# Attention with a routed mixture of experts: routing weights carried with the rows and applied to each expert tile's output

## The chip, the cores and the metric

The program runs on one core of one Trainium2 chip. The core has five engines that run side by side and meet only at semaphores: TensorE (PE, with its weight loads as PEld), VectorE (DVE), ScalarE (ACT), GpSimd (POOL) and SyncE (SP, which issues most transfers). The metric is the time in microseconds of one execution on the device; lower is better.

## The reference, cut to what matters

The input is 4 batches of 1,024 tokens with 256 values each. A layer norm gives `xn`. One branch is causal attention with 16 heads and a linear decay. The other is a mixture of 8 experts, of which each token takes two. The output is `x + s * silu(experts)`.

```python
probs = softmax(x @ gate_w)
gate_score, gate_idx = top_k(probs, 2)
gate_score = gate_score / sum(gate_score)
combine = einsum('tk,tke->te', gate_score, onehot) * alpha
h = gelu(einsum('th,ehi->eti', x, fc1_w) + fc1_b)
y = einsum('eti,eih->eth', h, fc2_w) + fc2_b
out = einsum('eth,te->th', y, combine)
...
x = x + s * silu(out)
```

So the sum over experts has two terms for each token, each the output of one chosen expert times one weight (`gate_score` times that expert's `alpha`).

## The kernel before, in words

**Three stages.** From the start to about 522 us the kernel does the layer norm, the projections and the attention, in 16 windows of four heads; beside the first windows it chooses the experts. From about 522 to 667 us it runs the experts. Until 710 us it adds up: the last projection of the attention, the two weighted expert rows of each token, silu, product, input.

**Routing and scatter (attention stage).** The 4,096 tokens are 32 tiles of 128. `weight[:, t, k]` holds the weight of the token's k-th expert, `slot[:, t, k]` the row of a sorted list in DRAM, `xs_dram`, in which the rows of one expert stand together and each expert begins at a multiple of 128 rows. GpSimd loads two or three token tiles into `x_move` (L897), writes the number of each row's place in `y_dram` into column 0 (L880), and sends one indirect DMA for each tile and k (L885): each row goes to its slot. A row of `xs_dram` is W = 257 words wide: the number, then the 256 values. `scatter(q, k)` paces these DMAs by the exponentials of the window q. The places between the experts' rows are cleared with a row `blank` whose number points to spare rows (`clear_pads`, L859).

**Experts.** There are SLOTS = 71 tiles of the sorted list. The order on each engine is written out by `skewed`: for each n it calls the named functions for tile n plus an offset.
- SP: `load_tile(n)` (L662 to L666) loads a tile into one of four buffers, when TensorE has transposed tile n - 4 and VectorE has taken its row numbers. SP's other loads and stores of this stage stand between these (L683 to L704).
- TensorE: `x_transpose(n + 3)` (L1677), `hidden(n + 2)` (L1694), `expert_out(n)` (L1716). `hidden` waits for the copied weights of the tile's expert (`w1_ready`), `expert_out` for gelu and for the output evacuation two tiles earlier (`y_out`).
- VectorE: `take_row(n + 3)` copies the column of row numbers into `y_row_of` (L1368); `h_evacuate(n + 2)` reads the tile's expert number into a register and adds that expert's bias while it moves the product from PSUM (L1374); `y_evacuate(n)` reads the number again and does the same for the second product into one of 8 buffers `ysb` (L1414). From tile 15 on, nine steps that split the output bias into three bfloat16 parts stand behind it (L1381 to L1400); tile 12 has an inversion of the attention's last sums before it.
- ScalarE: `x_evacuate(n + 3)` (L1009), `gelu(n + 2)` (L1013), `take_weights(n + 4)` (L1020), which copies the next expert's first weights.
- GpSimd: for each tile one indirect DMA from `ysb` to the rows of `y_dram` (L912), when `row_taken` and `y_out` allow. Beside 24 tiles (12 to 19, 31 to 38, 50 to 57) it first does one step of the attention's normalisation (`normalise`, L868), and eight such steps ahead of tile 0.

**Final sum.** SP waits until all stores to `y_dram` have landed, and then issues eight loads of `y`, each with the two expert rows of 256 tokens (0.52 MB), and further ones as `gsum_done` counts on; each output of 0.26 MB is stored behind `fin_done` (L715 to L720). There are 16 pairs of token tiles. For pair m:
- ScalarE: `scale_first(m)` multiplies the first row by its weight, two activations of 128x256 (L1040); `silu(m)` (L1046). `in_turn` sends `scale_first` two pairs ahead.
- VectorE: `add_second(m)` multiplies the second row by its weight and adds it, two instructions of 128x256 (L1429); `product(m)` multiplies with the attention's projection in PSUM (L1439); `add_input(m)` adds x (L1444). The order is `product(m)`, `add_second(m + 2)`, `add_input(m)`.
- TensorE: a bias matmul and eight more for each pair (L1737, L1742) into one of four banks, so it may be four pairs ahead of `product`.

## Time and profile before

| | |
|---|---|
| median of 3 runs | 706.29 us (703.04 to 708.08) |
| the profiled execution's own time | 712.01 us |
| its span | 710.2 us |
| granted TensorE clock, mean | 0.986 of full speed |
| busy: PE, PEld | 681.3 us, 451.7 us |
| busy: DVE, ACT, POOL | 536.2, 484.1, 239.9 us |
| packets of DMA | 74802, 124.46 MB |

The span is the profiled time from the first to the last instruction; the execution's own time has the work around it too. A row in the order of time gives the start in us, the duration in us, the engine, the line, the operation, what it writes `<-` what it reads, and in brackets how long the engine sat idle before and what ended that idle time. In the durations of VectorE the last 0.08 us or so overlap the next instruction if that has nothing to wait for, so the distance from start to start is what one costs. A time to landing counts from a transfer's issue to its last byte.

### The profile page before, as it was taken

The page shows a single profiled execution, that of the slowest core. Times are in us where ns is not written, and L with a number is a line of the kernel's source. Part 1 is how long each engine was busy: PE and PEld are TensorE (multiplying, and loading weights), DVE is VectorE, ACT ScalarE, POOL GpSimd, SP SyncE. Part 2 cuts the span into 40 slices and gives each one's busy share as a digit, 9 for nine tenths or more (in the row PEclk, how much of TensorE's full clock was granted, in tenths as well). Part 3 has the DMA queues.
Part 4 walks back from the last instruction along what each step waited for, and adds up shares of the span by engine and source line. Part 5 has one row for each costly group of instructions (what it writes and reads, how often), then busy time and mean ns, then how long its engine had stood idle before and what let it go on. Part 6 is the DMA issues. An engine that isn't in the chain of part 4 may idle for free.

```text
span 710.2 us, 16190 instructions
## 1 busy us (share of the span) xinstructions
PE 681.3 (96%) x5367; PEld 451.7 (64%) x5370; DVE 536.2 (75%) x1146; ACT 484.1 (68%) x994; POOL 239.9 (34%) x336
## 2 busy tenths in 40 slices
PE   7998999999999999999999999999999999999985
PEld 4876666455555555555555554554469999999764
DVE  6566887999999999989999899997234554444298
ACT  3553344577787877788787777778876666666374
POOL 4261211133023433324333342310025857575300
PEclk9999899899999999999999999999999999999999
DMA  6999885243776685676568558630179686955396
GB/s 206 279 270 376 251 282 194 55 66 89 105 138 142 136 175 130 134 183 132 145 153 180 132 115 171 151 68 18 48 183 279 243 205 214 237 177 179 117 399 248
DMA packets 74802, 124.46 MB, mean 175 GB/s; under 512 B 13832, under 2 KB 44296, under 8 KB 74600
## 3 DMA queue, kind: packets, MB, share of 16 engines
q1 hardware_dynamic: 65104, 95.26, 53.2%
q0 software_dynamic: 9616, 28.17, 13.1%
q8 instruction: 44, 0.72, 0.5%
q14 instruction: 38, 0.31, 0.2%
HBM read 72.64 MB, written 49.72 MB: 172 GB/s over the span
## 4 chain that ended last, share of the span: by engine, by line
PE 79%; DVE 9%; DMA 7%; ACT 2%; issue 2%; POOL 0%; POOLq 0%; SPq 0%; DVEq 0%; ACTq 0%
PE ps L1606 19%; PE ps L1590 14%; PE ps L1537 13%; PE ps L1694 9%; PE ps L1716 9%; PE ps L1526 6%; PE ps L1489 5%; DVE mxa L1131 3%; DMA aug<-q_parts 3%; PE ps L1499 2%; DMA q_parts<-arena 2%; PE ps L1677 2%; ACT arena L992 1%; DVE arena L1439 1%; DVE x_room L1444 1%
## 5 line engine op out<-in xcount | busy, mean ns | idle before, releaser
L1131 DVE TENSOR_REDUCE mxa<-ps 128x1 f32<-128x512 f32 (+3 forms) x608 | 358.1, 654 | 36.4 <-PE ps L1526 22.2
L992 ACT ACTIVATE arena<-ps 128x512 f32<-128x512 f32 x576 | 303.0, 606 | 78.2 <-PE ps L1590 42.2
L1590 PE MATMUL ps<-aug 59*128 59x512 f32 (+3 forms) x768 | 216.6, 402 | 0.8 <-ACT arena L992 0.5
L1537 PE MATMUL ps<-aug 57*128 57x512 f32 (+3 forms) x768 | 212.1, 401 | 4.9 <-DVE mxa L1131 1.9
L1590 PEld LDWEIGHTS ps<-aug 59*128 59x128 f32 x768 | 112.4, 188 | 78.8 <-ACT arena L992 70.2
L1606 PE MATMUL ps<-arena,v_q 128*32 128x512 f32 (+3 forms) x1536 | 155.5, 500 | 1.0 <-ACT arena L992 1.0
L1537 PEld LDWEIGHTS ps<-aug 57*128 57x128 f32 x768 | 109.4, 188 | 43.4 <-DVE mxa L1131 24.8
L885 POOL DMA_INDIRECT xs_dram<-arena,slot x64 | 62.7, 980 | 75.9 <-ACT arena L992 72.6
L912 POOL DMA_INDIRECT y_dram<-arena,y_row_of x71 | 69.6, 980 | 46.8 <-DVE y_row_of L1368 38.1
L1526 PE MATMUL ps<-key_mask,key_rows 64*128 64x128 bf16 (+2 forms) x352 | 76.9, 254 | 0.0
L1694 PE MATMUL ps<-arena 128*128 128x128 f32 x568 | 75.2, 275 | 0.0
L1526 PE MATMUL ps<-query_mask,query_rows 64*128 64x256 bf16 (+1 forms) x320 | 74.8, 260 | 0.0
L1716 PE MATMUL ps<-w_sb,arena 128*128 x284 | 73.1, 380 | 0.0
L1694 PEld LDWEIGHTS ps<-arena 128*128 128x128 f32 x568 | 69.1, 192 | 0.5 <-issue 0.4
L1374 DVE TENSOR_TENSOR arena<-ps,arena 128x256 f32<-128x256 f32 x71 | 30.2, 425 | 40.4 <-PE ps L1694 40.1
L1020 ACT ACTIVATE arena<-w_sb 128x512 f32 x69 | 43.5, 630 | 21.0 <-issue 19.6
L1606 PEld LDWEIGHTS ps<-arena,v_q 128*32 128x32 f32 x1536 | 34.9, 109 | 33.0 <-issue 18.3
L1489 PE MATMUL ps<-split_room 128*128 128x512 f32 x192 | 54.2, 418 | 1.1 <-DVE split_room L1190 1.1
L1414 DVE TENSOR_TENSOR arena<-ps,arena 128x256 f32<-128x256 f32 x71 | 30.1, 424 | 33.2 <-PE ps L1716 33.1
L1716 PEld LDWEIGHTS ps<-w_sb,arena 128*128 128x128 f32 x284 | 48.7, 191 | 4.3 <-issue 0.4
L1013 ACT ACTIVATE arena<-arena 128x256 f32<-128x256 f32 x71 | 29.6, 417 | 27.4 <-DVE arena L1374 27.4
L1526 PEld LDWEIGHTS ps<-key_mask,key_rows 64*128 64x128 bf16 x352 | 30.1, 94 | 18.1 <-issue 10.5
(150 smaller groups left out, 639.3 us busy)
## 6 DMA issues: line engine op xcount, KB each, us to landing
aug<-k_parts SPq DMA_DIRECT2D x96, 128.0 KB, 4.8
aug<-q_parts SPq DMA_DIRECT2D x96, 128.0 KB, 4.5
arena<-xs_dram SPq DMA_DIRECT2D x71, 128.5 KB, 3.3
k_parts<-arena SPq DMA_DIRECT2D x16, 512.0 KB, 5.0
q_parts<-arena SPq DMA_DIRECT2D x16, 512.0 KB, 5.4
arena<-y_dram SPq DMA_DIRECT2D x16, 512.0 KB, 7.8
xn_dram<-arena SPq DMA_DIRECT2D x8, 512.0 KB, 5.3
a_dram<-arena SPq DMA_DIRECT2D x128, 32.0 KB
```

The source lines that it names most:

```text
L885: nc.gpsimd.indirect_dma_start(out=xs_dram, in_=x_move[:, s, :], in_offset=None, out_offset=bass.IndirectOffsetOnAxis(ap=slot[:, first_til ...
L912: nc.gpsimd.indirect_dma_start(out=y_dram, in_=ysb[n % STEP], in_offset=None, out_offset=bass.IndirectOffsetOnAxis(ap=y_row_of[:, n:n + 1] ...
L992: nc.scalar.activation(prob_slot(q, i), score_bank(q, i), ACT.Exp).then_inc(exp_done, 1)
L1020: nc.scalar.activation(w1_now[j % 2], w1_sb[:, bass.ds(e * KT, KT), :], ACT.Copy).then_inc(w1_ready, 1)
L1131: nc.vector.tensor_reduce(dst, src, AX.X, ALU.max).then_inc(piece_used, 1)
L1489: ins = nc.tensor.matmul(bank(4 + n % 2), w[:, k, m * P:(m + 1) * P], xT[:, k, :], start=(s == 0 and k == 0), stop=(s == 2 and k == KT - 1))
L1526: return nc.tensor.matmul(bass.AP(out_.tensor, out_.offset + first, cols), stationary[rows, :, :].rearrange("p a two -> p (a two)"), over( ...
L1537: ins = nc.tensor.matmul(banks[:, at_ * width:(at_ + 1) * width], k_aug[n][rows, hp, ib * P:(ib + 1) * P], q_aug[n][rows, hp, lo:lo + widt ...
L1590: ins = nc.tensor.matmul(out_[:, col0:col0 + hi - lo], q_aug[n][rows, h // SIDES_OF_ARRAY, jb * P:(jb + 1) * P], k_aug[n][rows, h // SIDES ...
L1606: ins = nc.tensor.matmul(bank(OUT_BANK)[2 * HD * h:2 * HD * (h + 1), lo - c * BANK:BANK], v_q[n][:, jb, h, :], prob_slot(q, i)[:, col0:col ...
L1694: ins = nc.tensor.matmul(bank(2 + j % 2)[:, m * P:(m + 1) * P], w1_now[j % 2][:, k, m * P:(m + 1) * P], xgT[j % CH][:, k * P:(k + 1) * P], ...
L1716: ins = nc.tensor.matmul(bank(6 + j % 2)[:, 0:D], hid[j % CH][:, k * P:(k + 1) * P], w2_sb[:, e * KT + k, :], start=(k == 0), stop=(k == K ...
```

## The change

1. A row of `xs_dram` is 258 words wide (`LEAD = 2`): number, weight, 256 values. `scatter` copies the weights of its tiles into column 1 with one more GpSimd copy. The two clearing patterns cover the second column.
2. `take_row` copies two words. They go to `row_and_weight`, which lies in the memory of `logits`.
3. `h_evacuate` keeps the register with the tile's expert number for `y_evacuate`, which does not read it again.
4. `y_evacuate` counts a new semaphore `y_biased` with its addition, waits for it, and multiplies the tile in place by the row's weight; `y_out` now counts the multiplication. TensorE waits for `y_biased` (it needs the PSUM bank only), GpSimd's store for `y_out`.
5. In the final sum ScalarE no longer scales; VectorE adds the two rows of a pair with one tensor_tensor of 128x512 and waits for the load of `y` itself. `in_turn` and `y_scaled` are gone.

```diff
-W = D + 1
+LEAD = 2
+W = D + LEAD
...
             def scatter(q, k):
...
+                nc.gpsimd.tensor_copy(x_move[:, 0:count, 1:2], weight[:, first_tile:first_tile + count, k:k + 1]
+                                      ).then_inc(rows_ready, 1)
+                pool.wait_ge(rows_ready, 2 * (2 * r + k) + 3)
...
-                pool.wait_ge(y_out, n + 3)
+                pool.wait_ge(y_out, n + 1)
                 nc.gpsimd.indirect_dma_start(
                     out=y_dram, in_=ysb[n % STEP], in_offset=None,
-                    out_offset=bass.IndirectOffsetOnAxis(ap=y_row_of[:, n:n + 1], axis=0)).then_inc(y_stored[n % STEP], 16)
+                    out_offset=bass.IndirectOffsetOnAxis(ap=row_and_weight[:, n, 0:1], axis=0)).then_inc(y_stored[n % STEP], 16)
...
-            def scale_first(m):
-                j = m % DEEP
-                act.wait_ge(ya_in[m % DEEP_Y], 16 * (m // DEEP_Y) + 16)
-                if m >= DEEP:
-                    act.wait_ge(sg_done, m - DEEP + 1)
-                for i in range(2):
-                    ins = nc.scalar.activation(gsum[j][:, i * D:(i + 1) * D], ya[m % DEEP_Y][:, i, 0, :], ACT.Identity,
-                                               scale=weight[:, 2 * m + i, 0:1])
-                ins.then_inc(y_scaled, 1)
...
-            in_turn(scale_first, silu)
+            for m in range(NT // 2):
+                silu(m)
...
             def take_row(n, j):
                 dve.wait_ge(xg_in[j % CH], 16 * (n // CH) + 16)
-                nc.vector.tensor_copy(y_row_of[:, bass.ds(n, 1)], x_move[:, j % CH, 0:1].bitcast(i32)).then_inc(row_taken, 1)
+                nc.vector.tensor_copy(row_and_weight[:, n, :], x_move[:, j % CH, 0:LEAD].bitcast(i32)).then_inc(row_taken, 1)
...
             def h_evacuate(n, j):
-                e = dve.value_load(tile_expert[0:1, bass.ds(n, 1)], min_val=0, max_val=E - 1)
+                e = expert_of[n] = dve.value_load(tile_expert[0:1, bass.ds(n, 1)], min_val=0, max_val=E - 1)
...
-                e = dve.value_load(tile_expert[0:1, bass.ds(n, 1)], min_val=0, max_val=E - 1)
+                e = expert_of.pop(n)
                 dve.wait_ge(l2_done, n + 1)
                 if n >= STEP:
                     dve.wait_ge(y_stored[j % STEP], 16 * (n // STEP))
-                nc.vector.tensor_tensor(ysb[j % STEP], bank(6 + j % 2)[:, 0:D], b2_sb[:, e, :], ALU.add).then_inc(y_out, 1)
+                nc.vector.tensor_tensor(ysb[j % STEP], bank(6 + j % 2)[:, 0:D], b2_sb[:, e, :], ALU.add).then_inc(y_biased, 1)
+                dve.wait_ge(y_biased, n + 3)
+                nc.vector.tensor_scalar(ysb[j % STEP], ysb[j % STEP], row_and_weight[:, n, 1:2].bitcast(fp32), None,
+                                        ALU.mult).then_inc(y_out, 1)
...
             def add_second(m):
                 j = m % DEEP
-                dve.wait_ge(y_scaled, m + 1)
-                for i in range(2):
-                    part = gsum[j][:, i * D:(i + 1) * D]
-                    ins = nc.vector.scalar_tensor_tensor(part, ya[m % DEEP_Y][:, i, 1, :], weight[:, 2 * m + i, 1:2],
-                                                         part, ALU.mult, ALU.add)
-                ins.then_inc(gsum_done, 1)
+                dve.wait_ge(ya_in[m % DEEP_Y], 16 * (m // DEEP_Y) + 16)
+                if m >= DEEP:
+                    dve.wait_ge(sg_done, m - DEEP + 1)
+                nc.vector.tensor_tensor(gsum[j].rearrange("p (t d) -> p t d", d=D), ya[m % DEEP_Y][:, :, 0, :],
+                                        ya[m % DEEP_Y][:, :, 1, :], ALU.add).then_inc(gsum_done, 1)
...
-                pe.wait_ge(y_out, n + 1)
+                pe.wait_ge(y_biased, n + 1)
```

## Rows read from the trace of the kernel before

**Rows 1.** The page's head and its busy time by engine (busy us, share, instructions).

```profile
span 710.2 us, 16190 instructions
...
PE 681.3 (96%) x5367; PEld 451.7 (64%) x5370; DVE 536.2 (75%) x1146; ACT 484.1 (68%) x994; POOL 239.9 (34%) x336
```

**Rows 2.** Busy time by stretch, expert stage: columns PE, PEld, DVE, ACT, POOL busy, PEclk, DMA share, GB/s.

```profile
560.00:600.00 40.00, 40.00 (x284) 36.93 (x283) 20.80 (x69) 26.72 (x62) 27.06 (x31) 1.00 0.72 202
```

**Rows 3.** Order of time in the expert stage: start us, us, engine, line, operation, idle before.

```profile
600.64 0.42 DVE L1414 TENSOR_TENSOR arena<-ps,arena 128x256 f32<-128x256 f32 x1 [0.44 <-PE ps L1716]
600.88 0.74 POOL L868 TENSOR_TENSOR v_all<-v_all,arena 128x256 f32<-128x256 f32 x1
...
600.98 0.14 DVE L1368 COPY y_row_of<-arena 128x1 int32<-128x1 int32 x1
...
601.75 0.42 DVE L1374 TENSOR_TENSOR arena<-ps,arena 128x256 f32<-128x256 f32 x1 [0.63 <-PE ps L1694]
601.83 1.01 POOL L912 DMA_INDIRECT y_dram<-arena,y_row_of  x1 [0.21 <-issue]
...
602.62 0.42 DVE L1414 TENSOR_TENSOR arena<-ps,arena 128x256 f32<-128x256 f32 x1 [0.44 <-PE ps L1716]
...
602.92 0.63 ACT L1020 ACTIVATE arena<-w_sb 128x512 f32 x1 [0.29 <-issue]
...
604.49 1.06 PE L1694 MATMUL ps<-arena 128*128 128x128 f32 x8
```

**Rows 4.** Busy time by stretch, final stage.

```profile
685.00:690.00 5.00, 5.00 (x24) 3.78 (x23) 5.00 (x12) 3.79 (x9) 0.00 (x0) 1.00 1.06 395
```

**Rows 5.** Order of time in the final stage, all engines.

```profile
668.36 1.89 PE L1742 MATMUL ps<-wo_sb,v_all 128*128 128x256 f32 x8
...
673.86 0.91 ACT L1040 ACTIVATE arena<-arena,weight 128x256 f32<-128x256 f32 x2 [8.64 <-DMA arena<-y_dram]
...
676.94 0.68 DVE L1439 TENSOR_TENSOR arena<-ps,arena 128x512 f32<-128x512 f32 x1
...
700.93 0.68 DVE L1439 TENSOR_TENSOR arena<-ps,arena 128x512 f32<-128x512 f32 x1
...
701.53 0.86 DVE L1429 SCALAR_TENSOR_TENSOR arena<-arena,weight 128x256 f32<-128x256 f32 x2
702.32 0.68 DVE L1444 TENSOR_TENSOR x_room<-x_room,arena 128x512 f32<-128x512 f32 x1
...
702.92 0.68 DVE L1439 TENSOR_TENSOR arena<-ps,arena 128x512 f32<-128x512 f32 x1
```

**Rows 6.** The line of GpSimd's row-number copies: duration ns min/median/max.

```profile
L880 POOL COPY arena<-y_row x22: 188/191/215, 180.9 to 456.7; 128x3 int32<-128x3 int32 x20, 128x2 int32<-128x2 int32 x2
```

**Rows 7.** Order of time of VectorE, tile that also splits the output bias.

```profile
568.14 0.42 DVE L1374 TENSOR_TENSOR arena<-ps,arena 128x256 f32<-128x256 f32 x1 [0.29 <-PE ps L1694]
```

**Rows 8.** Groups of VectorE instructions by shape: count | busy us, mean ns | idle before.

```profile
L1351 DVE COPY arena<-w_sb 128x512 f32 x2 | 0.9, 430 | 5.9 <-issue 5.9
...
L1180 DVE TENSOR_SCALAR arena<-arena,rstd,shift 128x256 f32<-128x256 f32 x2 | 0.7, 410 | 0.0
...
L1392 DVE CAST arena<-arena 128x256 bf16<-128x256 f32 x1 | 0.4, 417 | 0.0
...
L1386 DVE CAST arena<-ob_sb 128x256 bf16<-128x256 f32 x1 | 0.3, 284 | 0.0
```

**Rows 9.** The line of the tile loads (L666), of the loads issued from 579 to 582.

```profile
DMA to landing us min/median/max: 6.6/6.6/6.6
```

**Rows 10.** Order of time at the end of the expert stage.

```profile
663.70 0.42 DVE L1414 TENSOR_TENSOR arena<-ps,arena 128x256 f32<-128x256 f32 x1 [0.44 <-PE ps L1716]
...
664.88 0.96 POOL L912 DMA_INDIRECT y_dram<-arena,y_row_of  x1 [0.79 <-DVE arena L1414]
...
667.41 0.96 POOL L912 DMA_INDIRECT y_dram<-arena,y_row_of  x1 [0.30 <-issue]
```

**Rows 11.** The line of the loads of y (L706), all 16.

```profile
DMA to landing us min/median/max: 3.8/7.8/9.3
```

More of the change, by code:

```diff
@@ L227, in is_last @@
     return isinstance(q, int) and q == NQ - 1
-def in_turn(ahead, what):
-    for m in range(AHEAD_OF_PRODUCT):
-        ahead(m)
-    for m in range(NT // 2):
-        what(m)
-        if m + AHEAD_OF_PRODUCT < NT // 2:
-            ahead(m + AHEAD_OF_PRODUCT)
 def attention_moe_kernel(nc, x, wqT, wkT, wvT, woT, qb, kb, vb, ob, gate, w1, b1, w2, b2, alpha,
@@ L297, in attention_moe_kernel @@
         tile_expert = sb("tile_expert", [P, SLOTS], i32)
-        y_row_of = sb("y_row_of", [P, SLOTS], i32)
+        row_and_weight = logits[:, :, :].rearrange("p t e -> p (t e)")[:, 0:LEAD * SLOTS].bitcast(i32).rearrange("p (n r) -> p n r", r=LEAD)
         y_row = sb("y_row", [P, NT, 2], i32)
         blank = sb("blank", [P, W])
-        zeros = blank[:, 1:W]
+        zeros = blank[:, LEAD:W]
         pad_slot = sb("pad_slot", [P, E], i32)
@@ L304, in attention_moe_kernel @@
         spare = sb("spare", [P, E, 2], i32)
-        ARENA = 16 * 1024 + CH
+        ARENA = 16 * 1024 + LEAD * CH
         arena = sb("arena", [P, ARENA])
@@ L361, in attention_moe_kernel @@
         at[0] = 0
-        xg = [x_move[:, j, 1:W] for j in range(CH)]
+        xg = [x_move[:, j, LEAD:W] for j in range(CH)]
         at[0] = 0
@@ L461, in attention_moe_kernel @@
         g_done = sem("g_done"); w1_ready = sem("w1_ready"); l2_done = sem("l2_done")
-        y_out = sem("y_out"); y_stored = [sem(f"y_stored{n}") for n in range(STEP)]
+        y_biased = sem("y_biased"); y_out = sem("y_out"); y_stored = [sem(f"y_stored{n}") for n in range(STEP)]
         x_all_in = sem("x_all_in"); a_in = [sem(f"a_in{b}") for b in range(B)]
         ya_in = [sem(f"ya_in{n}") for n in range(DEEP_Y)]
-        vb_turned = sem("vb_turned"); vb_out = sem("vb_out"); vb_done = sem("vb_done"); ob_step = sem("ob_step"); ob_split = sem("ob_split"); s_proj = sem("s_proj"); y_scaled = sem("y_scaled")
+        vb_turned = sem("vb_turned"); vb_out = sem("vb_out"); vb_done = sem("vb_done"); ob_step = sem("ob_step"); ob_split = sem("ob_split"); s_proj = sem("s_proj");
         gsum_done = sem("gsum_done"); silu_done = sem("silu_done"); sg_done = sem("sg_done")
@@ L490, in many_zeros @@
         def many_zeros(n):
-            return bass.AP(zeros.tensor, zeros.offset, [list(zeros.ap[0]), [0, n], [1, D]])
+            first = blank[:, 1:W]
+            return bass.AP(first.tensor, first.offset, [list(first.ap[0]), [0, n], [1, W - 1]])
         best, first, second, gap, gexp, where, norm, low = col
@@ L725, in _ @@
         def _(pool):
-            nc.gpsimd.memset(zeros, 0.0).then_inc(zeros_set, 1)
+            nc.gpsimd.memset(blank[:, 1:W], 0.0).then_inc(zeros_set, 1)
             for n in range(AUG):
@@ L896, in _ @@
                     first_tile, count = MOVES[r], MOVES[r + 1] - MOVES[r]
-                    pool.dma_start(x_move[:, 0:count, 1:W], xn_t[:, first_tile:first_tile + count, :]).then_inc(x_moved, 16)
+                    pool.dma_start(x_move[:, 0:count, LEAD:W], xn_t[:, first_tile:first_tile + count, :]).then_inc(x_moved, 16)
                 next_v(q, q % AUG)
@@ L1054, in _ @@
             dve.sem_inc(h_out, 2)
-            dve.sem_inc(y_out, 2)
+            dve.sem_inc(y_biased, 2)
             def statistics(i, b, c):
@@ L1367, in take_row @@
                 dve.wait_ge(xg_in[j % CH], 16 * (n // CH) + 16)
[L1368 removed]
+                nc.vector.tensor_copy(row_and_weight[:, n, :], x_move[:, j % CH, 0:LEAD].bitcast(i32)).then_inc(row_taken, 1)
+            expert_of = {}
             def h_evacuate(n, j):
[L1372 removed]
+                e = expert_of[n] = dve.value_load(tile_expert[0:1, bass.ds(n, 1)], min_val=0, max_val=E - 1)
                 dve.wait_ge(l1_done, n + 1)
@@ L1728, in _ @@
             skewed(((x_transpose, 3), (hidden, 2), (second_expert, 0), (expert_out, 0)), 0)
-            pe.wait_ge(y_out, SLOTS + 2)
+            pe.wait_ge(y_biased, SLOTS + 2)
             pe.wait_ge(ob_split, NBIAS)
```

1 line of the change is left out of this document (removed).

## The prediction

> **What bounds the kernel now.** The page's first part says TensorE is busy 96% of a span of 710.2 us, VectorE 75%, ScalarE 68% and GpSimd 34% [rows 1]. That is a mean over three stages (attention to about 522 us, experts to 667, the final sum to 710), and the change touches almost nothing in the first, so the views to read are those of the other two.
>
> In the expert stage the busy time by stretch shows TensorE without a gap, 40.00 us of 40, while VectorE has 20.8 [rows 2]. The order of time shows one tile: VectorE's y evacuation starts at 600.64 and the next at 602.62, a period of 1.98 us, each having waited 0.44 us for TensorE's second matmul; the h evacuation between them at 601.75 waited 0.63 us for the first [rows 3]. TensorE alone sets this stage: what is added to VectorE costs nothing until something that TensorE needs is late.
>
> In the final stage VectorE is busy 5.00 us of 5. TensorE shows 5.00 too, but its records stretch over waits (it is four banks ahead, and the rows of VectorE show no wait for it), and the DMA engines move 395 GB/s with a share over 1 [rows 4]. The order of time shows VectorE's loop: product at 700.93, two scaled adds from 701.53, input added at 702.32, next product at 702.92: 0.60 + 0.79 + 0.60 = 1.99 us, none with an idle time [rows 5]. So VectorE sets that stage and the DMA engines stand right behind it.
>
> **The change, part by part.** *Scatter rows (attention).* 22 more GpSimd copies of 128x3, each 0.19 us as the one beside it [rows 6], 4 us in all, with GpSimd at 34% [rows 1] and its scatters paced by waits for ScalarE's exponentials. The next scatters and the reload of the rows queue behind each copy, and have windows of over 20 us. If that cover were gone it would be 4 us; I take 0. Rows of 1,032 bytes for 1,028 add 0.4% to the scatters, the tile loads and the pad writes: 0.
>
> *Row taken per tile.* Two elements for one in a 0.14 us copy [rows 3]: 0.
>
> *Expert number read once.* The h evacuation at 568.14 follows the row copy after 0.29 us [rows 7]; the read lies in that gap, so a read costs at most 0.29 us of VectorE. 71 of them go, but each lies in the 0.44 us that VectorE waits for TensorE: 0. What it does is to make room.
>
> *Multiply per tile.* It is a tensor_scalar, 128x256 float32 in SBUF, with a scalar per partition. The nearest row is exactly that form: 0.410 us (two of them, L1180) [rows 8]. The lower bound is the cast at 0.284 us, where one source streams faster; I take 0.41, plus some 0.04 us until the evacuation before it has landed, together 0.45. The Trainium skill ("VectorE: DVE Perf Modes", the perf-mode tier table) has a float32 tensor_scalar in SBUF at two elements a cycle, like a copy. By that rule the multiply would take some 0.28 us and the sum would be 0.13 us lower. The trace disagrees for the form with pointer scalars: 0.410 us, where a copy of twice the elements took 0.430 [rows 8].
>
> Does it fit? VectorE's loop becomes: evacuation until it has landed 0.46, multiply until the next can start 0.34 (an evacuation at 600.64 lets the row copy start at 600.98), row copy and read 0.14 + 0.30, h evacuation 0.34: 1.58 us of 1.98 [rows 3, 7]. The margin is 0.40. The h evacuation moves from 1.11 us behind the y evacuation to 1.24, 0.13 late. Behind it on ScalarE stand gelu and the copy of the next expert's weights, which starts at 602.92, takes 0.63 us and is wanted by TensorE at 604.49 [rows 3]: slack 0.94. The next y evacuation is not moved. Tiles 15 to about 26, which also split the output bias (another 0.34 us), make a loop of 1.92 and a lateness of 0.47, still under both. Tile 12, which also inverts sums, is later than these once: a stall of 0 to 0.2 us.
>
> *The load behind the row.* SP queues its tile load behind the row copy, now 0.45 us later, and so all that SP issues after it. It is for the tile four loops on, whose transposes come just ahead of the h matmuls that follow those of 604.49 [rows 3] by two periods, 608.3: it has some 6.8 us. The longest, of the stretch from 579 us, took 6.6 [rows 9]: these tiles may stall TensorE by 0.2 us. I take 0.2 for the stage; its bounds are 0 and 1.
>
> *GpSimd's store per tile.* It now waits for the multiply. In the stretches where it also normalises, its own work is 0.74 + 1.01 us and a gap [rows 3], just under 1.98; starting 0.45 us later does not lengthen it, and the eight buffers take the shift. But at the end of the stage it counts. The evacuation at 663.70 ends at 664.12, and the store that waited for it starts at 664.88; the last starts at 667.41, 2 x 1.27 us behind, back to back [rows 10]. The third last store therefore shifts in full and with it the last, the loads of y and all that follows: **+0.45 us**.
>
> *The final stage.* ScalarE's two scalings per pair go, as do VectorE's two scaled adds; one tensor_tensor of 128x512 comes. The input add of the same form, both sources in SBUF, keeps VectorE for 0.60 us (702.32 to 702.92) [rows 5]. The period becomes 0.60 + 0.60 + 0.60 = 1.80, against 1.99. 14 of the 16 loops hold an add: 14 x 0.19 = **-2.7 us**. At the start, the first load lands at 673.86, where ScalarE now begins; the first product is at 676.94 [rows 5]. New: the first add at 673.9, the second when the second load lands (0.52 MB at 395 GB/s [rows 4] take 1.3 us: 675.2), the product 0.60 later at 675.8, and some 0.1 us lost to the third load: **-1.0 us**. The silu takes 0.63 us and has ended by then.
>
> What is late next? TensorE's projection of a pair, eight matmuls over 1.89 us and one ahead of them [rows 5], takes at most 2.1 us against 1.80, but it starts four pairs ahead: 7.2 us of lead, less the product's 0.68 and its own 2.1, leaves 4.4, of which at most 12 x 0.3 = 3.6 are used. A load of y is issued behind the store of pair m-9 and wanted six loops and a product later, 11.4 us; it took 7.8 in the median, 9.3 at most [rows 11]. Of the 12.6 MB of loads and stores at most 12.1 are left when the first load lands, 30.6 us at 395 GB/s [rows 4]: 704.5 at the latest, and earlier by what the next loads had moved by then. VectorE, whose last product and add are behind the loop, would end at 703.9, both plus the shift. The transfers just about fit.
>
> **Sum:** +0.2 + 0.45 - 2.7 - 1.0 = -3.1 us. The profiled execution took 712.0 (span 710.2), so 708.9 for it; it stands 5.7 above the median of the runs, 706.3, from which I count: **703.2**.
>
> **Rivals.** *Transfers set the final stage.* For it: 395 GB/s and a share over 1 now [rows 4], and 0.786 MB a pair need 1.97 us at 400 GB/s, more than 1.80. Against it: eight loads are out ahead, and the last stores no longer share the engines with loads. Then only the earlier start stays, and a little of the period: -0.5 in all, 705.8. Chance 0.17.
>
> *The expert stage slows (the slower side).* The mechanism: the multiply and a GpSimd instruction exclude each other, so that the multiply waits for a GpSimd instruction to end. For it: of two casts of one shape to bfloat16 in this stage, one took 0.284 and one 0.417 us [rows 8], and GpSimd is busy 1.75 us of 1.98 while it normalises [rows 3]. Against it: the 0.41 form suggests the slow way of streaming, and the 0.417 may be just that. It decides from a wait of 0.40 us a tile. If each multiply waited for a store of 1.01 us, the loop would be 1.58 + 1.01 - 0.13 = 2.46, 0.48 too long, in the 24 tiles beside a normalisation: +11.5, so 706.3 - 3.1 + 11.5 = 714.7. Chance 0.08. The Trainium skill ("SBUF — State Buffer", Who interferes with whom) states this exclusion for a VectorE instruction in a two-port mode. With a multiply in the slow mode it would not arise; no row here shows it for certain.
>
> *VectorE or the tile loads are late more often than counted*, say 0.3 us in ten tiles of the busy stretch: 706.2. Chance 0.06. For it: loads of 6.6 us [rows 9]. Against it: TensorE shows no gap where they were.
>
> **How the numbers follow.** My forecast has 0.64, the transfers 0.17, late loads 0.06, the exclusion 0.08; 0.05 is for a gain beyond the sum that I can't name. A difference under 1% (7 us) cannot be told from no change here, as the three runs span 703.0 to 708.1. So: faster 0.05, same 0.87, slower 0.08. The terms reach from -4.2 (a cheap multiply, no stall) to +0.5 (transfers set the pace, stalls of 1 us), and the median of three runs moves by another 1 to 2: 700.3 to 707.6.
>
> **What would show it.** Right: TensorE still 40 of 40 in the expert stage, period 1.98; multiply near 0.41; the h evacuation 1.24 behind the y evacuation; the first load of y issued 0.45 later against TensorE's last matmul; products 1.80 apart, adds without an idle time; last store about 3 us earlier. Wrong: adds that wait for transfers (first rival); gaps of TensorE beside normalisations and multiplies of over 0.5 us (second); a multiply of 0.28; or a stage period that TensorE's projection sets.

## The result and the profile after

| | before | changed |
|---|---|---|
| median of 4 runs | 707.18 us (703.04 to 711.57) | 714.11 us (710.42 to 719.21) |
| profiled execution, span | 712.01, 710.2 us | 710.42, 708.6 us |

Ratio 1.0080 with a 95% interval of 1.0042 to 1.0118: slower by 6.9 us, where 3.1 us of gain were forecast. The trace does not show that loss: its span is 1.6 us shorter. The marks of the stages, from the lines of the second matmul and of the loads of y:

| us | before | changed |
|---|---|---|
| start to the first second matmul | 526.6 | 523.5 |
| first to last second matmul (expert stage) | 138.6 | 142.8 |
| last second matmul to first load of y | 4.8 | 5.3 |
| first load of y to the end (final stage) | 40.2 | 37.0 |

The first line is no effect of the change: it was 521.3 in another execution of the kernel before, and over all traces of this document it is 521.3 to 526.6 without the wider rows and 522.3 to 524.5 with them on chips where the kernel before takes about 707 us, 533.1 to 533.8 and 531.4 to 535.4 where it takes 721. The other three are, and give +4.2 + 0.5 - 3.2 = **+1.5 us**.

**Expert stage.** Busy time by stretch, kernel after (columns as in [rows 2]):

```profile
560.00:600.00 40.00, 39.75 (x276) 35.84 (x275) 31.47 (x88) 26.12 (x60) 26.44 (x29) 1.00 0.73 196
600.00:640.00 40.00, 39.51 (x278) 35.73 (x277) 29.34 (x80) 25.77 (x60) 26.05 (x29) 1.00 0.77 201
```

TensorE is no longer without a gap, and carries 276 groups of matmuls where [rows 2] has 284. VectorE went from 20.8 to 31.5 us. What TensorE waits for, from the list of waits (us in total, times, longest):

```profile
PEld ps L1666 <- DMA arena<-xs_dram: 5.3, 9, 1.3
PE ps L1666 <- DMA arena<-xs_dram: 1.9, 4, 0.9
```

The weight loads of the transposes (L1666) waited 5.3 us for tile loads, in nine tiles; before, 0.7 in one (the second row has the matmuls' part of the same waits). Here is one such load, in order of time: the engines' rows, then the piece of the chain of waits.

```profile
612.62 0.42 DVE L1401 TENSOR_TENSOR arena<-ps,arena 128x256 f32<-128x256 f32 x1 [0.32 <-PE ps L1705]
613.08 0.35 DVE L1403 TENSOR_SCALAR arena<-arena,logits 128x256 f32<-128x256 f32 x1
613.35 0.16 DVE L1353 COPY logits<-arena 128x2 int32<-128x2 int32 x1
```

```profile
612.04 0.91 SPq L602 DMA_DIRECT2D arena<-inv_dram  x2
613.00 0.43 SPq L670 DMA_DIRECT2D x_room<-in_x  x1
613.59 2.31 SPq L658 DMA_DIRECT2D arena<-xs_dram  x2
```

```profile
619.55 1.03 PE L1705 MATMUL ps<-w_sb,arena 128*128 x4
621.07 0.44 PE L1666 MATMUL ps<-idf,arena 128*128 128x128 f32 x2 [0.49 <-DMA arena<-xs_dram]
```

```profile
613.59 7.44 DMA arena<-xs_dram
```

The evacuation starts at 612.62, the row copy 0.73 us behind it where it was 0.34 [rows 3], and the load at 613.59. It is issued behind two loads of the attention's inverse sums (L602, 128 KB each, into 16 partitions) and one of x (L670), and lands 7.44 us later; the transpose at 621.07 waited for it. The same load of the kernel before left at 613.39 and those of 613 to 619 took 4.5 to 5.1 us. Of the tile loads whose landing the list knows, the longest took 8.5 us (6.6 before). The transposes of tiles 11 to 13, 33 and 50 held the stage up by 0.3 to 1.1 us each. In every trace that has such waits, of either kernel, they stand at the same few tiles: at 4, whose load SP issues right behind the first eight loads of inverse sums, and ahead of the first multiply; at 11 to 14, 32 and 33, and 48 to 51, near the other loads of inverse sums; and at 19.

**Beside a normalisation** VectorE looks otherwise (order of time, VectorE, GpSimd and SP):

```profile
600.76 0.42 DVE L1401 TENSOR_TENSOR arena<-ps,arena 128x256 f32<-128x256 f32 x1 [0.19 <-PE ps L1705]
601.22 0.40 DVE L1403 TENSOR_SCALAR arena<-arena,logits 128x256 f32<-128x256 f32 x1
601.54 0.69 DVE L1353 COPY logits<-arena 128x2 int32<-128x2 int32 x1
602.15 0.41 DVE L1361 TENSOR_TENSOR arena<-ps,arena 128x256 f32<-128x256 f32 x1
602.74 0.42 DVE L1401 TENSOR_TENSOR arena<-ps,arena 128x256 f32<-128x256 f32 x1 [0.18 <-PE ps L1705]
```

```profile
601.42 0.78 POOL L860 TENSOR_TENSOR v_all<-v_all,arena 128x256 f32<-128x256 f32 x1
```

```profile
602.31 2.30 SPq L658 DMA_DIRECT2D arena<-xs_dram  x2
```

The copy of two words takes 0.69 us and ends at 602.23, as GpSimd's tensor_tensor does at 602.20; in [rows 3] one word took 0.14 in the same place. Still VectorE waits 0.18 us for TensorE in each of these tiles, so here it is not the bound. But the tile load that waits for the copy leaves 1.55 us behind the evacuation, where it was 0.77 (601.41 against 600.64). The two lines over all tiles:

```profile
L1403 DVE TENSOR_SCALAR arena<-arena,logits x71: 352/354/965, 525.2 to 667.3; 128x256 f32<-128x256 f32 x71
```

```profile
L1353 DVE COPY logits<-arena x71: 150/163/697, 520.9 to 661.9; 128x2 int32<-128x2 int32 x71
```

The multiply is 0.354 us in the median, not 0.41.

**In tiles 15 to 20 VectorE is the bound.** There normalisations, multiplies and the steps that split the output bias fall together. Rows in order of time and the stretch from 560 us, kernel after:

```profile
559.85 0.41 DVE L1361 TENSOR_TENSOR arena<-ps,arena 128x256 f32<-128x256 f32 x1
560.19 0.41 DVE L1401 TENSOR_TENSOR arena<-ps,arena 128x256 f32<-128x256 f32 x1
560.63 0.69 DVE L1403 TENSOR_SCALAR arena<-arena,logits 128x256 f32<-128x256 f32 x1
...
563.23 0.81 DVE L1373 CAST arena<-ob_sb 128x256 bf16<-128x256 f32 x1
...
565.22 0.95 DVE L1376 TENSOR_TENSOR arena<-ob_sb,arena 128x256 f32<-128x256 f32 x1
```

```profile
560.00:570.00 10.00, 10.00 (x68) 8.81 (x67) 9.80 (x26) 6.51 (x15) 8.23 (x10) 1.00 0.51 152
```

The same two steps and the same stretch, kernel before:

```profile
563.41 0.28 DVE L1386 CAST arena<-ob_sb 128x256 bf16<-128x256 f32 x1
...
565.39 0.41 DVE L1389 TENSOR_TENSOR arena<-ob_sb,arena 128x256 f32<-128x256 f32 x1
```

```profile
560.00:570.00 10.00, 10.00 (x72) 9.23 (x71) 5.98 (x20) 6.71 (x17) 8.60 (x10) 1.00 0.49 158
```

The y evacuations of tiles 15 and 20 are 10.46 us apart instead of 9.89, and VectorE has 0.18 us of idle time between them instead of 3.91. TensorE shows no gap here, but carries 68 groups of matmuls for 72. From the second matmul of tile 14 to that of tile 28 the stage takes 0.7 us more than 14 periods of 1.977 us (0.0 before), and no load is waited for there. Below this is called the loss of tiles 14 to 28.

**End of the stage and final stage** (order of time, the rows that answer to [rows 10] and [rows 5]):

```profile
664.67 0.96 POOL L906 DMA_INDIRECT y_dram<-arena,logits  x1 [1.02 <-DVE arena L1403]
...
669.01 0.96 POOL L906 DMA_INDIRECT y_dram<-arena,logits  x1 [0.30 <-issue]
...
671.61 4.29 SPq L698 DMA_DIRECT2D arena<-y_dram  x8
...
675.81 0.69 DVE L1419 TENSOR_TENSOR arena<-arena 128x512 f32<-128x512 f32 x1 [8.19 <-DMA arena<-y_dram]
```

```profile
699.66 0.68 DVE L1428 TENSOR_TENSOR arena<-ps,arena 128x512 f32<-128x512 f32 x1
700.27 0.68 DVE L1419 TENSOR_TENSOR arena<-arena 128x512 f32<-128x512 f32 x1
700.87 0.69 DVE L1433 TENSOR_TENSOR x_room<-x_room,arena 128x512 f32<-128x512 f32 x1
701.47 0.68 DVE L1428 TENSOR_TENSOR arena<-ps,arena 128x512 f32<-128x512 f32 x1
```

Products 699.66 and 701.47: a period of 1.80 us against 1.99, no idle time. Neither TensorE nor the transfers set it, at

```profile
685.00:690.00 5.00, 5.00 (x25) 4.13 (x24) 5.00 (x9) 1.65 (x3) 0.00 (x0) 1.00 1.06 392
```

### The profile page after: what moved, and what is told of

The parts are those of the page before. It is cut to its first block, busy times and chain, and to the rows that moved or that the text cites. A ratio compares the mean times of both kernels' runs of the same rounds, so it can differ in the third digit from the quotient of the medians.

```text
span 708.6 us, 16025 instructions
## 1 busy us (share of the span) xinstructions
PE 681.6 (96%) x5370; PEld 451.7 (64%) x5370; DVE 571.0 (81%) x1201; ACT 471.4 (67%) x962; POOL 242.8 (34%) x358
## 4 chain that ended last, share of the span: by engine, by line
PE 78%; DVE 9%; DMA 7%; ACT 2%; issue 2%; POOL 0%; SPq 0%; DVEq 0%; POOLq 0%; ACTq 0%
PE ps L1595 19%; PE ps L1579 14%; PE ps L1526 13%; PE ps L1683 8%; PE ps L1705 7%; PE ps L1515 6%; PE ps L1478 5%; DMA arena<-xs_dram 3%; DVE mxa L1116 3%; PE ps L1488 3%; DMA q_parts<-arena 3%; PE ps L1666 2%; ACT arena L986 1%; DVE x_room L1433 1%; DVE arena L1428 1%
## 5 line engine op out<-in xcount | busy, mean ns | idle before, releaser
L906 POOL DMA_INDIRECT y_dram<-arena,logits x71 | 69.5, 979 | 51.6 <-DVE logits L1353 47.2
```

The source lines that it names most:

```text
L906: nc.gpsimd.indirect_dma_start(out=y_dram, in_=ysb[n % STEP], in_offset=None, out_offset=bass.IndirectOffsetOnAxis(ap=row_and_weight[:, n, ...
```

## The experiments

The theory after this result (A): the row copy stands behind the multiply, so tile loads leave later than their landing time allows, and TensorE waits. Rivals: (B) VectorE is held by GpSimd beside the normalisations; (C) the multiply or the wider rows cost by themselves; (D) the 0.8% of the first comparison is no effect of the change. Below, "stage" is the time from the first to the last second matmul, and "waits" the time for which the weight loads of the transposes waited for tile loads (0.7 in the profile before, 5.3 in that of after). The kernel before took 721.06 and 720.72 us on the chip of e1 to e8, 720.83 on that of e13 to e16, 708.80 on that of e9 to e12.

**e1: the changed kernel again.** No edit.

> The changed kernel once more, nothing edited, so that the experiments beside it are measured against it on one chip. In its first trace the final stage ran in 37.0 us from the first load of y to the end (40.2 before), the expert stage from the first to the last second matmul took 142.8 us (138.6 before), and TensorE waited for tile loads that landed after 7.3 to 8.5 us. Theory A (late tile loads cost the expert stage more than the final stage gives): 142 to 148 us in the expert stage, 37.0 in the final one, time 1.003 to 1.012 of before. Rival (the difference lies in the attention stage, which the change only touches with GpSimd copies and wider rows): expert stage 139 to 142 us, first second matmul later than 527 us.

721.11 us, ratio 0.9980 (0.9952 to 1.0009). Stage 145.0, waits 3.0, final stage 37.2. The slowdown is not repeated, though the stage is as long as theory A has it: D gains. But 2.7 of the 3.0 us of waits are tile 4's, whose load left at 530.87, ahead of the first multiply (534.97), and behind that wait the granted clock was 0.75 from 535 to 540: the multiply's lateness can't have made this part.

**e2: two copies of one word.**

```diff
-nc.vector.tensor_copy(row_and_weight[:, n, :], x_move[:, j % CH, 0:LEAD]...)
+nc.vector.tensor_copy(row_and_weight[:, n, 0:1], x_move[:, j % CH, 0:1]...)
+nc.vector.tensor_copy(row_and_weight[:, n, 1:2], x_move[:, j % CH, 1:2]...).then_inc(row_taken, 1)
```

> The row number and the weight are taken by two copies of one word each instead of one copy of two. Theory (the two-word copy excludes GpSimd's instructions, 0.69 us beside a normalisation against 0.16): each copy takes 0.10 to 0.15 us everywhere, also beside normalisations, the h evacuation again waits for TensorE there, the stalls on tile loads shrink somewhat, expert stage 139 to 142 us, time 1 to 3 us under e1. Rival (any VectorE copy from SBUF waits for GpSimd): the copies still take 0.5 us or more beside normalisations and the time is that of e1. Rival (lateness from the multiply alone, 0.46 us a tile, sets the stalls): copies short, time within 1 us of e1.

720.54 us, 0.9981 (0.9958 to 1.0005). Stage 143.3, waits 2.6 us. Beside GpSimd's normalisation:

```profile
609.63 0.38 DVE L1404 TENSOR_SCALAR arena<-arena,logits 128x256 f32<-128x256 f32 x1
609.92 0.14 DVE L1353 COPY logits<-arena 128x1 int32<-128x1 int32 x1
609.99 0.14 DVE L1354 COPY logits<-arena 128x1 int32<-128x1 int32 x1
```

```profile
609.81 0.78 POOL L860 TENSOR_TENSOR v_all<-v_all,arena 128x256 f32<-128x256 f32 x1
```

One word is never held, two words are. But the time is that of e1: this hold is real and not what costs.

**e3: the next row copy ahead of the multiply.**

```diff
                 nc.vector.tensor_tensor(ysb[j % STEP], ...).then_inc(y_biased, 1)
+                if n + CH < SLOTS:
+                    take_row(n + CH, (n + CH) % STEP)
                 dve.wait_ge(y_biased, n + 3)
```

> The two-word row copy of the next tile stands between the output evacuation and the multiply instead of behind the multiply, so SP may issue the tile load 0.4 us earlier, as in the kernel before. Theory A (tile loads issued too late): TensorE waits under 1 us for loads, expert stage 138.6 to 140 us, time 3 to 5 us under e1, so 0.994 to 0.999 of before. Rival (the exclusion of GpSimd and VectorE, not the loads): the copy keeps its 0.69 us beside normalisations and the expert stage stays at 142 us or more.

722.45 us, 1.0034 (1.0008 to 1.0061). Slower, against A's forecast. Stage 146.1, waits 3.7. The edit does what it should: from the y evacuation to the tile load behind it 0.72 us pass in the mean of all tiles, against 1.28 in e1 and 0.64 in e9, the kernel before; at most it is 1.1, where GpSimd holds the copy. So the loads leave almost on time and the stage is no shorter, which A can't explain. Two things stand against the edit's gain: where VectorE waits for a landing in take_row (once, 1.6 us), all behind it now waits too, and the loss of tiles 14 to 28 is 1.2 us. The longest wait is tile 50's, whose load landed 9.7 us after its issue. One late load costs more than its wait (busy time by stretch):

```profile
625.00:630.00 5.00, 2.92 (x18) 2.04 (x16) 2.09 (x6) 2.59 (x6) 1.91 (x2) 1.00 1.05 287
630.00:635.00 5.00, 4.69 (x23) 4.24 (x24) 1.66 (x6) 1.81 (x4) 0.96 (x1) 0.66 0.37 124
```

TensorE's matmuls stop from 628.1 to 630.3, and in the stretch after that its granted clock is 0.66 of full speed in the mean, so partly 1.2 GHz; four matmuls of the second layer take 1.90 us instead of 1.03. This is one execution; it explains part of this stage's length, not of all.

**e4: the final sum alone.** The kernel before with part 5 of the change: the experts' outputs are added without their weights, which nothing applies.

> The kernel before with the new final sum alone: one tensor_tensor of 128x512 a pair, no scaling on ScalarE; no weight column and no multiply, so the weights are left out. All theories expect the expert stage of before (138.6 us) and the last second matmul to first load of y at 4.8 us as before. My step of the sum: final stage 36.5 us from the first load of y to the end against 40.2, time 3 to 4 us under before, ratio 0.995. Rival (transfers set the final stage): 39 us or more, ratio 0.999 to 1.000.

716.69 us, 0.9947 (0.9927 to 0.9968). Stage 140.1, waits 0.6, final stage 36.4. The half of the change that should gain gains 0.5%.

**e5: a fifth tile buffer.** The changed kernel with the tile loads in five buffers; the fifth is free memory of a weight matrix used earlier.

```diff
-                if n >= CH:
-                    sp.wait_ge(row_taken, n - CH + 1)
-                sp.dma_start(x_move[:, j, :], ...)
+                if n >= XB:
+                    sp.wait_ge(row_taken, n - XB + 1)
+                sp.dma_start(x_row[j], ...)
```

> The changed kernel with a fifth buffer for expert tiles (in the memory of the query weights, dead by then), so that SP may issue each tile load one tile, 1.98 us, earlier; nothing else differs. Theory A (the expert stage of the changed kernel is long because its tile loads are issued too late for their landing time): TensorE waits under 1 us for loads beyond the first tiles, expert stage 138.5 to 140.5 us instead of 142.8 to 146, final stage 37, time 0.990 to 0.995 of before. Rival (the exclusion between VectorE and GpSimd holds the expert stage): waits for loads shrink but the stage stays over 142 us, ratio 0.998 to 1.003.

719.44 us, 0.9967 (0.9948 to 0.9986): the first version with the whole computation that beats both kernels, by less than A asked for. Stage 141.8, where A had at most 140.5. Two waits for tile loads are left (1.0 and 0.5 us), and one that a fifth buffer can't touch:

```profile
PEld ps L1668 <- DMA wq_sb<-xs_dram: 1.0, 1, 1.0
...
PEld ps L1668 <- DMA arena<-xs_dram: 0.5, 1, 0.5
```

```profile
547.23 0.42 DVE L1403 TENSOR_TENSOR arena<-ps,arena 128x256 f32<-128x256 f32 x1 [3.26 <-PE ps L1707]
```

This is the y evacuation of tile 4. It waits for no store, as the eight buffers are first used again at tile 8. Its second matmuls are recorded from 543.04, but the signal of their end came at 547.09; what held it back the trace does not show. At tile 8 the stage is 1.7 us late by it. e4 (0.5) and e15 (1.2) have such a lateness too, so the change did not bring it, and no trace has it from a chip on which the kernel before takes about 707 us. The loss of tiles 14 to 28 stays at 0.7.

**e6 and e7: no hold by GpSimd**, with five buffers and with four. The one-word copies of e2; and the sum with the bias stays in PSUM, from where the multiply reads, so TensorE gets the bank back only behind the multiply.

```diff
-nc.vector.tensor_tensor(ysb[j % STEP], bank(6 + j % 2)[:, 0:D], b2_sb[:, e, :], ALU.add)
+nc.vector.tensor_tensor(bank(6 + j % 2)[:, 0:D], bank(6 + j % 2)[:, 0:D], b2_sb[:, e, :], ALU.add)
-nc.vector.tensor_scalar(ysb[j % STEP], ysb[j % STEP], ...)
+nc.vector.tensor_scalar(ysb[j % STEP], bank(6 + j % 2)[:, 0:D], ...)
```

> As e5, and no VectorE instruction of the tile loop can use both SBUF ports: row number and weight in two one-word copies, and the bias addition writes back to PSUM, from where the multiply reads. Theory A: the same as e5 within 1 us. Rival (exclusion): 2 us or more faster than e5. Both: the multiply takes 0.42 us or a little more everywhere, never 0.9.

722.03 us, 1.0020 (0.9997 to 1.0043); stage 142.1, waits 0.3.

> The changed kernel with four buffers as it is, and the two edits against the exclusion alone: two one-word copies, multiply out of PSUM. Theory A (late loads): the row copies are still 0.4 to 0.5 us later than before, so the waits for loads stay at 3 us or more and the time is 0.996 to 1.000 of before. Rival (exclusion): expert stage under 140.5 us and 0.990 to 0.995 of before.

720.99 us, 1.0006 (0.9976 to 1.0036); stage 144.3, waits 2.8. With the hold of these instructions gone the waits of four buffers remain: B is out as the main cause, and e6 against e7 again shows 2.2 us less with the fifth buffer. B is not out altogether: the steps of the bias split can still be held (0.82 us for a subtraction in e7), and the loss of tiles 14 to 28 is 0.8 us in e6 and 1.0 in e7. Why e6 is slower than e5 with a stage of the same length its trace does not show.

**e8: weights carried, not used.** The changed kernel with e2's copies and without the multiply.

> The changed kernel with two one-word copies and without the multiply per tile: the weights travel but are never applied (that part of the result is left out). Theory A: row copies come as early as before, so the expert stage is that of before and of e4, 138.5 to 140.5 us, last second matmul to first load of y 4.8 us, ratio 0.994 to 0.996. Rival (the wider rows or the copies in the attention stage cost time): ratio 0.998 or more with the expert stage at 140.

718.99 us, 0.9976 (0.9954 to 0.9997); stage 142.0, waits 2.4. This run too speaks against A as the whole account. Without the multiply the row copies are only 0.07 us later than before, and still the stage is 2.2 us above the mean of e4, e15, e9 and the profile before (139.8), and the gain half of e4's. It is one trace, and those four differ by 2.1 among themselves. e2, which adds the multiply to it, has 1.3 us more. But that is no price of the carrying (wider rows, the second word, the copies ahead of the scatters): 1.9 us of e8's stage are the lateness at tile 4 that e5 has too, which is 0, 0, 0.5 and 1.2 us in the other four. What the run does show is in tiles 14 to 28: without the multiply the loss there is 0.0.

**e9: the kernel before against itself**, as a measure of the comparison.

> The kernel before, nothing edited, for a trace on the chip of the other experiments. All theories: the same time as before. Expected stages if the chip and not the change explains the longer times here: first second matmul near 533 us (526.6 in the first trace of before), expert stage 139 to 141 us, 4.8 us to the first load of y, final stage 40 us.

707.95 us, 0.9984 (0.9955 to 1.0014); stage 139.7, waits 2.0, final stage 40.5. Tile loads make the kernel before wait too, in some executions more than in that of the profile I read.

**e10 and e11: no loads of inverse sums**, in the changed kernel and in the one before. Those loads (L602) and the normalisation are left out.

> The changed kernel without the 32 loads of the inverted sums in the expert stage and without GpSimd's 32 normalisation steps (so the attention branch is left unnormalised). Theory A' (the later row copies hurt only because tile loads land late, and they land late only beside these loads): TensorE waits under 0.5 us for tile loads, expert stage 138.5 to 139.5 us, and against the same edit of the kernel before (e11) it is 2.5 to 3.5 us faster, the sum of my final stage and end of stage. Rival (VectorE's own longer loop holds the stage): still over 141 us.

706.29 us, 0.9967 (0.9943 to 0.9992); stage 138.1. The tile loads, and the transposes' list of what they waited for:

```profile
DMA to landing us min/median/max: 1.9/2.3/5.2
...
L1662 PE MATMUL ps<-idf,arena x142: 272/273/330, 519.8 to 657.2; 128*128 128x128 f32 x142
its engine sat idle before it (us, times) until:
  issue: 0.2, 1
```

> The kernel before with the same two things left out. All theories: expert stage 138.3 to 139 us, final stage 40.2, so its time is at most 2 us under before; it is the base for e10.

707.74 us, 0.9974 (0.9947 to 1.0002); stage 138.2. Without these neighbours the two kernels' stages are equal, 138.1 and 138.2, with all multiplies in place. So the loss needs the inverse sums' loads or the normalisation. For the waits e7 speaks against the normalisation's hold; in tiles 14 to 28, where e10 loses 0.0 us, it is the normalisation that is missing, as VectorE's own work is the same. The gain of e10 over e11 is 1.5 us, less than the 2.5 to 3.5 that were expected; in the two traces the first second matmul comes at 524.5 and 523.1, within the spread of that mark.

**e12: fifth buffer and one-word copies**, on this second chip.

> The changed kernel with the fifth tile buffer of e5 and the two one-word copies of e2; the multiply stays in SBUF. Candidate for the best version. Theory A: 0.993 to 0.997 of before, expert stage 140 to 142 us, at most 1 us from e5. Rival (the two-word copy's wait for GpSimd matters on its own): 1 us or more faster than e5.

707.03 us, 0.9993 (0.9966 to 1.0020); stage 139.7, waits 1.4. The gain of e5 is not confirmed by it; its interval overlaps e5's.

**e14: the kernel before, plus the multiply.** Each tile is multiplied by a column of ones, and the second read of the expert number stays. The final sum is that of before.

```diff
                 e = dve.value_load(tile_expert[0:1, bass.ds(n, 1)], min_val=0, max_val=E - 1)
...
-nc.vector.tensor_tensor(...).then_inc(y_out, 1)
+nc.vector.tensor_tensor(...).then_inc(y_biased, 1)
+dve.wait_ge(y_biased, n + 3)
+nc.vector.tensor_scalar(ysb[j % STEP], ysb[j % STEP], vone[:, 0:1], None, ALU.mult).then_inc(y_out, 1)
```

> The kernel before with one part of the change alone: each output tile is multiplied in place by a column of ones, with the two semaphores of the change. The final sum, the rows and the one-word copies are those of before. Theory A: expert stage 141 to 144 us with 3 us or more of waits for tile loads, end of stage 5.3 us, final stage 40.2, ratio 1.003 to 1.008. Rival (the multiply is hidden): expert stage 138.6 to 140, ratio 1.000 to 1.001.

734.85 us, 1.0198 (1.0163 to 1.0233); stage 155.1. VectorE has become the bound. One tile from the chain that ended last (DVEq is VectorE's sequencer; L1375 and L1413 are the two reads):

```profile
640.13 0.42 DVE arena L1417
640.59 0.31 DVE arena L1419
640.90 0.10 DVE y_row_of L1371
641.00 0.12 DVEq L1375
...
641.35 0.33 DVE arena L1377
641.71 0.19 DVEq L1413
...
642.20 0.43 DVE arena L1417
```

From 640.13 to 642.20 VectorE alone takes 2.07 us, more than TensorE's 1.98. From the h evacuation (641.35) to the y evacuation 0.85 us pass; in the changed kernel, where nothing is waited for, 0.34 (559.85 to 560.19, above). So the second read costs 0.51 us.

**e13, e15 and e16: the changed kernel, the final sum alone, the changed kernel**, beside e14 on a third chip.

> The changed kernel, nothing edited. Theory A (final stage and end of stage -3.0 us as in the sum, expert stage longer by 3 to 5 us from tile loads that are issued later and land late beside the inverse loads): expert stage 141 to 145 us, ratio 0.998 to 1.006. Rival (the first comparison was right and holds more than the expert stage): 1.006 or more.

719.89 us, 1.0006 (0.9984 to 1.0027); stage 144.6, waits 5.3 in five tiles, the longest 2.2.

> As e4, on the chip of this call: the kernel before with the new final sum alone (weights left out). All theories: expert stage as before, final stage 36.5, ratio 0.994 to 0.996. Rival (transfers): 0.999 or more.

717.07 us, 0.9949 (0.9930 to 0.9969); stage 140.7, waits 2.0.

> The changed kernel a second time in this call, to see how much two looks at one kernel differ. Theory A and rival as for e13; the two should agree within 0.3%, and their expert stages within 3 us.

719.88 us, 0.9993 (0.9970 to 1.0016); stage 141.8, waits 1.9. The same kernel as e13, with 2.8 us less in its stage: how late the loads are varies from one execution to the next.

## Why the prediction was wrong

**The step that failed** is "The load behind the row": a stall of 0.2 us for the stage, with bounds 0 and 1. The stage took 138.6, 139.7, 140.1 and 140.7 us in the four traces with a one-word copy and no multiply (before, e9, e4, e15), and 142.8, 145.0, 144.6 and 141.8 in the four of the changed kernel: 139.8 and 143.6 in the mean, **+3.8 us**; chip by chip 138.6 and 139.7 against 142.8, 140.1 against 145.0, 140.7 against 144.6 and 141.8. I had the lateness right at 0.45 us away from normalisations (0.40 more from evacuation to load) and only half of it beside them (0.78). What I mis-sized was the margin, on both sides. The room is 6.4 us and not 6.8: in e16 the load of tile 48 was issued at 618.71 and its transpose was ready for it at 625.1. And I took one longest landing, 6.6 us, and called the rest of the loads safe. Landings reached 8.5 us in the changed kernel and 7.4 in e9, the kernel before, which waited 2.0 us where my profile had 0.7. The margin was gone before the change came.

**A second step failed beside it**, "Does it fit?". I had a loop of 1.92 us for tiles 15 to about 26, with 0.34 us for a step of the bias split, "still under both". Beside GpSimd's normalisations those steps took 0.81 and 0.95 us and the multiply up to 0.965, and in tiles 15 to 20 VectorE set the pace. The loss of tiles 14 to 28 is 0.7, 0.7, 1.4 and 0.7 us in the four traces of the changed kernel (in the 1.4 lies a wait of 0.75 for tile 19's load) and 0.0, 0.0, 0.0 and 0.4 in the other four (the 0.4 has such a wait too). It is 0.0 without the multiply (e8) and 0.0 without the normalisation (e10), so it takes both.

What the runs show and what they don't: the waits for tile loads were 0.7, 2.0, 0.6 and 2.0 us in the first four traces and 5.3, 3.0, 5.3 and 1.9 in the others, 1.3 and 3.9 in the mean, so they are 2.6 of the 3.8 us, and VectorE's tiles 15 to 20 are 0.7. The waits vanish with the inverse sums' loads and the normalisation (e10 against e11), and a fifth buffer makes them fewer (e5). That the multiply's lateness is their whole cause is not shown. Tile 4's load is issued ahead of every multiply; without this tile the waits are 0.7 us in the mean of the first four traces and 2.8 in the others. And e3 and e8, whose loads leave less than 0.1 us later than before, waited 3.7 and 2.4 us, because single loads took 9.7 and 8.4 us. What lengthens a landing is open, and so is what the carrying adds.

**Expert number read once.** Right in effect (0), wrong in price: I had bounded a read at 0.29 us from [rows 7]; it costs 0.51. In the kernel before 0.87 us pass from the h evacuation to the y evacuation (601.75 to 602.62 [rows 3]), and VectorE alone needs 0.85 for that (e14): the 0.44 us of idle time that the row puts down to TensorE were mostly the read itself, not a reserve. With the multiply it no longer fits: e14 against e13, on one chip, is 155.1 against 144.6 us of stage. "It makes room" was the sentence that carried the change, and it deserved a number: 71 x (2.07 - 1.98) is 6.4 of those 10.5 us. For the rest there are two candidates in e14's trace, which were not taken apart: its multiply is 0.438 us in the mean from 560 to 640, since GpSimd holds it beside normalisations, and the transposes of tile 19 waited 2.7 us for their load, behind which TensorE's granted clock was 0.79 and 0.87 in the two stretches from 570 to 580.

**Multiply.** 0.41 forecast, 0.354 measured; the distance to the next instruction is 0.27 us (613.08 to 613.35). The Trainium skill ("VectorE: DVE Perf Modes", the perf-mode tier table) was right that this form streams two elements a cycle, and I was wrong to read 0.410 us [rows 8] as the slow way: cast 0.284, one pointer scalar 0.354, two pointer scalars 0.410, all of 256 elements. Some 0.06 us for each pointer scalar would fit the three, which differ in more than that (the cast writes bfloat16, the last form has two operations). The loop takes 1.80 us of 1.98 around 601 us; in tiles 15 to 20 it does not fit, as said above.

**Row copy.** Forecast 0, measured 0.16 us, and 0.69 beside GpSimd's tensor_tensor. It cost VectorE's margin and a later load, but no time that e2 could find.

**End of the stage.** Forecast +0.45, measured +0.5: right.

**Final stage.** Forecast -3.7, measured -3.2. The period is 1.80 as forecast. From the first load of y to the first product it is 6.1 against 6.9 us (-0.8 for -1.0), and from the first to the last product 26.9 against 29.3 (-2.4 for -2.7): two later adds waited 0.8 us for their loads. e4 and e15 give -0.5% for this half by itself, 3.8 and 3.7 us.

**The rivals.** *Transfers set the final stage*: refuted by the period of 1.80. *The exclusion*: the hold is real. By the Trainium skill ("SBUF — State Buffer", SBUF: two separate sides) it takes a VectorE instruction in a two-port mode, or one with two inputs in SBUF; the traces agree, with the multiply stretched to 0.965 us at most and the subtraction of the bias split (two inputs in SBUF) to 0.95. It is part of the 0.7 us of tiles 15 to 20, far from the +11.5 of the rival: elsewhere VectorE kept a wait of 0.18 us a tile. *Late loads*: its mechanism is the one that was found, but priced at +3.0 us over the forecast, 706.2; by the later comparisons that price was nearly right (0.9980 to 1.0006 are 704.9 to 706.7 us on the scale of before), and the chance of 0.06 was too small. Those times lie in my range of 700.3 to 707.6, but by its width: the stage was 3.6 us off. Its ends were also summed loosely: a cheap multiply without a stall gives -3.4 and not -4.2 us, the transfers' -0.5 with a stall of 1 us +0.3 and not +0.5.

**What stays open.** The sum by these traces is +3.8 + 0.5 - 3.2 = +1.1 us, and the three later comparisons, 36 runs, found 0.9980, 1.0006 and 0.9993. The first found 1.0080 from four runs of each kernel, and its own trace does not show where 7 us would be. The changed kernel was not run again on a chip on which the kernel before takes 707 us, so a part that belongs to such a chip is not excluded; e12, the changed kernel with two edits, shows none there (0.9993). I would call the change worth nothing either way: half a percent gained in the final sum, and about as much lost in the expert stage.

## What to carry to other kernels

A pipeline whose profile already shows one wait for a load (here 0.7 us) has no margin in that place: don't price a later issue from the longest landing of one trace, for a second execution of the same kernel waited 2.0 us. Check the fit of a loop in the few tiles where all side work meets, with each instruction at the length it has beside the other engines: the mean tile here had room, tiles 15 to 20 had none. When work is put behind an evacuation, look at what other queue waits for the small instruction that follows it: here 0.4 us on an idle VectorE made a transfer late that is wanted four tiles on. An instruction that costs nothing because it hides in an idle gap gets its full price back as soon as something else fills the gap, and a gap in a list of waits may be no gap at all: register reads are not counted as busy.

## What the runs showed of the hardware that I had not expected

- A VectorE copy of two 4-byte words in SBUF is held until a running GpSimd tensor_tensor ends (0.16 us free, 0.69 us held); one word is not (0.14 us at all times, e2). The Trainium skill ("VectorE: DVE Perf Modes", What auto-detection actually checks) gives the two-port mode to an instruction whose single source and destination are in SBUF with outermost non-unit dimensions both even or equal. Two words meet that and one word has no such dimension; the traces agree with this reading.
- Reading a register on VectorE between two instructions adds 0.51 us start to start (0.85 in e14, 0.34 without it), more than a 128x256 evacuation's own 0.34.
- The same multiply from PSUM takes 0.484 us, from SBUF 0.354, and is then never stretched by GpSimd (482 to 485 ns over 71 tiles in e7).
- After TensorE had matmuls missing for 2.2 us (e3), its granted clock was 0.66 in the mean of the next 5 us, so partly 1.2 GHz. Behind a gap of 2.3 us it was 0.75 (e1) and 0.79 (e14, gap at 570 us). After a gap of 1.8 us in e13 it stayed at 1.00.
- Tile loads of 129 KB landed after 1.9 to 5.2 us, 2.3 in the median, where the loads of inverse sums and GpSimd's normalisation are left out (e10), and after up to 8.5 us with them.
